# Latent attention: the first half of the next tile's scores ahead of the turning of the current tile's weights

## The reference

```python
C_q  = Q @ Wq_d                                   # 512 -> 64
C_kv = K @ Wkv_d                                  # 512 -> 32
CqWqk = (C_q @ W_qk).reshape(b, n, 16, 32)        # 16 heads
scores = einsum('bnhl,bkl->bhnk', CqWqk, C_kv) / sqrt(32)
attn = softmax(scores)
V_up = (C_kv @ Wv_u).reshape(b, nkv, 16, 32)
out  = einsum('bhnk,bkhd->bnhd', attn, V_up)      # then x = x + tanh(g_xattn[2]) * out
```

## Time and profile before

| what | value |
|---|---|
| median of 3 runs | 2076.41 us (2075.19 to 2080.06) |
| profiled execution: time, span | 2071.11 us, 2069.4 us |
| PE, DVE, ACT, POOL busy over the span | 90%, 79%, 28%, 32% |
| PE, DVE busy of the 1047 us of the first three layers | 907.78 us, 791.88 us |
| latent attention of turn 0: its first exponentials to the last tile's weighted values | 252.33 to 280.19 us |
| waits of ACT's L1188 for DVE's L1630 | 70.0 us in 16 |

### The profile page before, as it was taken

One profiled execution on the slowest core, in us unless ns is written; L12 is line 12 of the kernel. 1 busy time (PEld: TensorE's weight loads), 2 busy tenths in 40 slices (PEclk: granted clock), 3 DMA queues, 4 the chain that ended last, 5 costly groups with the idle time before them and its releaser, 6 DMA issues. The chain is left out here.

```text
span 2069.4 us, 37628 instructions
## 1 busy us (share of the span) xinstructions
PE 1862.5 (90%) x15007; PEld 1043.4 (50%) x15007; DVE 1632.1 (79%) x2908; ACT 586.7 (28%) x1347; POOL 656.3 (32%) x786
## 2 busy tenths in 40 slices
PE   8788889989899898998866899999999999999987
PEld 6344556446554466444533455555555555555543
DVE  4689676986679866798744888888888888888895
ACT  3312233222332223222324122222222222222343
POOL 3500233011420104201124443434343434344563
PEclk9899999999999989999967999999999999999998
DMA  8657204461145601454032211111111111111011
GB/s 245 184 174 211 65 1 144 135 193 41 42 124 156 192 1 42 124 173 113 1 138 72 67 52 47 52 42 52 52 52 52 52 52 52 52 27 32 16 42 52
DMA packets 142300, 176.50 MB, mean 85 GB/s; under 512 B 46768, under 2 KB 82768, under 8 KB 142000
## 3 DMA queue, kind: packets, MB, share of 16 engines
q1 hardware_dynamic: 140112, 172.88, 28.5%
q10 hardware_dynamic: 2016, 1.22, 0.3%
HBM read 131.98 MB, written 42.08 MB: 84 GB/s over the span
## 5 line engine op out<-in xcount | busy, mean ns | idle before, releaser
L1311 POOL TENSOR_TENSOR early_vare<-early_mv,w_eps 128x1 f32<-128x1 f32 x96 | 30.2, 315 | 734.2 <-DVE early_mv L1395 724.3
L2452 POOL TENSOR_TENSOR la_q<-la_straight,la_rot 128x512 f32<-128x512 f32 x128 | 163.3, 1276 | 163.9 <-DVE la_rot L2522 163.9
L440 PE MATMUL la_ps<-w_xTh,w_wqh 128*128 128x512 bf16 x512 | 197.3, 385 | 14.3 <-POOLq L116 8.1
L441 PE MATMUL la_ps<-w_xTl,w_wqh 128*128 128x512 bf16 x512 | 195.8, 382 | 0.0
L442 PE MATMUL la_ps<-w_xTh,w_wql 128*128 128x512 bf16 x512 | 195.7, 382 | 0.0
L440 PE MATMUL la_ps<-w_woh,la_oTh 128*128 128x512 bf16 x512 | 194.0, 379 | 0.0
L441 PE MATMUL la_ps<-w_wol,la_oTh 128*128 128x512 bf16 x512 | 194.0, 379 | 0.0
L442 PE MATMUL la_ps<-w_woh,la_oTl 128*128 128x512 bf16 x512 | 194.0, 379 | 0.0
L2465 POOL TENSOR_TENSOR la_p<-la_s,la_rec 128x256 f32<-128x256 f32 x128 | 90.2, 704 | 273.6 <-DVE la_rec L2543 273.6
L2384 ACT ACTIVATE la_oTh<-la_ps 128x256 bf16<-128x256 f32 x256 | 84.1, 380 | 294.4 <-PE la_ps L2267 294.4
L1552 DVE TENSOR_TENSOR early_products<-early_pR,early_vR 128x4096 f32<-128x4096 f32 x32 | 140.0, 4416 | 16.3 <-DMA early_pR<-scr_p 16.3
(11 more groups left out here) (355 smaller groups left out, 4627.2 us busy)
## 6 DMA issues: line engine op xcount, KB each, us to landing
early_vR<-scr_v SPq DMA_DIRECT2D x128, 257.0 KB, 5.3
early_wkv<-wkv SPq DMA_DIRECT2D x32, 512.0 KB, 4.3
la_v<-v SPq DMA_DIRECT2D x64, 256.0 KB, 4.0
k<-early_ctxt SPq DMA_DIRECT2D x32, 256.0 KB, 3.8
v<-early_ctxt SPq DMA_DIRECT2D x64, 128.0 KB, 2.5
scr_p<-early_weights SPq DMA_DIRECT2D x16, 512.0 KB, 5.0
early_pR<-scr_p SPq DMA_DIRECT2D x32, 256.0 KB, 3.8
w_raw_q<-in_Wq SPq DMA_DIRECT2D x8, 1024.0 KB, 7.5
```

Of the source, the lines that this page charges most:

```text
L440: pe.matmul(out, lh[c], rh[c], start=(first and c == 0), stop=False)
L441: pe.matmul(out, lh[c], rl[c], start=False, stop=False)
L2452: rope_sum.send(pool.tensor_tensor(dst, straight[:, slot, :], rot[:, slot, :], ALU.add))
```

## The change

In each of the three passes j = 0, 1, 2 in each of the four turns, PE issues `scores(j + 1, 0)` ahead of `turn_weights(j)` and no longer behind it. `turn_weights(j)` is now followed directly by `attend(j)`. Nothing else is added or taken away, and every wait stands with its block.

```diff
@@ -1022,9 +1022,9 @@
                         low(j + 2)
                     else:
                         idle_products(6, turn, "prob2", j, 0)
-                    turn_weights(j)
                     if j + 1 < QUAD:
                         scores(j + 1, 0)
+                    turn_weights(j)
                     attend(j)
                     if j + 1 < QUAD:
                         scores(j + 1, 1)
```

## The result

The changed kernel takes 2080.75 us (median of 20 runs, 2074.66 to 2087.59), the one before 2076.49 us beside it (20 runs, 2068.94 to 2080.36 but for one of 9434.22, whose cause is not on record; without it the median is 2076.41). The ratio is 1.0027, with a 95% interval of 1.0017 to 1.0037: slower by 5.6 us, with 3.5 to 7.7 in the interval. Forecast were 2085.8 us and slower by 9.4. The direction is right and the stall is where it was said to be; the amount is smaller than the sum.

What follows compares the result with a forecast made beforehand. DVE and PE were taken as nearly level, PE becoming the bound in tile 2. The tiles' delays reach +2.35 us a turn, 9.4 us over four turns, on the median 2076.41: 2085.8 us, range 2078.5 to 2091.

Steps and rivals of the forecast that it cites:

- Nothing to gain on DVE: In the loop's passes: the first half of the scores already stands before DVE wants it, so bringing it earlier wins nothing.
- The stall of a neighbouring pair: Transposes directly followed by `attend` take 1.98 us start to start against PE's own 0.97: a 1.01 us stall, 12 times.
- Tile 0, +0.44: In tile 0, DVE's second reduction waits for the later second half of the scores: 259.11 instead of 258.67, +0.44 us.
- Tile 1, +0.78 in all: In tile 1, the stall hides from DVE's division, but late scores add 0.10 us to the 0.68 carried in, +0.78.
- Tile 2, +2.35: In tile 2, PE becomes the bound and its 0.41 us slack goes: DVE reduces at 276.25 against 273.90, +2.35 us.
- A sign of the profile that did not come: DVE's reduction waiting for the scores (L977) in tiles 0 to 2, least in tile 1, over 1 us in tile 2.
- Four alike turns: The four turns are alike, so each loses the same 2.35 us, 9.4 us in all.
- I see no transfer that would hide it: Behind `attend(3)`, from layer norm to next turn, engines wait in a chain, so each turn's 2.35 us passes on whole.
- the clock as 3 us either way around nothing: Which block meets a fall of PE's clock from 2.4 to 1.2 GHz shifts, moving the total by 3 us either way.
- Rival A: In the loop, new 1 us gaps drop PE to 1.2 GHz: some 12 us on top, 2098 us; chance 0.05.
- Rival B: In the loop, DVE's own work hides the stall, leaving only 1.8 us in total: 2078.2 us; chance 0.12.
- Rival C: In tile 2, earlier scores fill PE's 0.41 us wait, gaining 1.6 us over four turns: 2072 to 2075; chance 0.05.

## Why the prediction was right, and where its size was off

- **Nothing to gain on DVE.** Right: the first scores half was never waited for before, and is not now.
- **The stall of a neighbouring pair.** Right: 1.98 forecast from tile 3's rows, 1.99 to 2.00 measured, 12 new waits of 0.90.
- **Tile 0, +0.44.** The reduction moved from 258.67 - 252.33 = 6.34 behind the first exponentials to 6.80: +0.46. **Tile 1, +0.78 in all:** 14.65 to 15.55, +0.90. The pair took 2.00 and not 1.98, and `low(3)` held PE for 1.56 (261.16 to 262.72) where I took 1.47. **Tile 2, +2.35:** 21.57 to 24.13, +2.56; the unused products took PE some 1.39 where I took 1.31 (from 268.89 + 1.02 = 269.91, the end of `up`, to 271.30). The loops' 10.3 us lie just above the 8.6 to 10.0 that I gave as bounds: those let only the unused products vary.
- **A sign of the profile that did not come.** DVE's reduction in tile 2 was to wait over 1 us for the scores; it waited 0.28. By my own times the division ends at 275.25 + 0.75 = 276.00, and the scores were to be read from 276.25. The long wait is the division's (1.23, forecast 1.3).
- **Four alike turns.** Right, 2.56 or 2.57 each.
- **"I see no transfer that would hide it", and the clock as 3 us either way around nothing.** This step failed in size. The sum took everything outside the loops as unchanged on the mean, 9.4 us, and measured were 5.6. At an equal mean clock the loss is 8 to 10 us, so the loops' term stands, and a term of about -4 us is missing: PE's mean clock is higher in the changed kernel. The sign of this term could not be had from the rows I used, which showed the clock at one place of one turn. `attend(3)` at 1.69 was in them, and I read it as a risk to the change instead of a cost that the kernel before already bore. That 2080.75 lies inside the range is owed to the 3 us of clock and the room towards B, not to the sum; and that it meets the 2080.5 I had from the profiled execution is luck.
- **Rival A** (the clock falls in the loop) is refuted: the granted clock is 1.00 in all four loops of both profiles of the changed kernel, and filling the stall changed nothing. The rule of the Trainium skill that I named for it ("TensorE: Matmul & The Clock Gate", "A second HAM failure mode: psum-queue depth-cycling") does not bite here, on gaps of 0.90 that stand 8.6 to 8.7 us apart. **Rival B** is refuted by the loops' 2.57. That its 2078.2 lies nearer to 2080.75 than my 2085.8 does is luck; its slack does exist (tile 1's division was not late), but only once a turn. **Rival C** is refuted by the 0.90.

Why the changed kernel meets a higher clock is not settled. The time that PE stood at 1.2 GHz, added up from the granted clock of stretches of 2 us, is 196 and 188 us in the two profiles of before and 183 and 176 us in those of the changed kernel. Only part of this lies right behind the loops, where the clock fell in 4 of 8 turns and in 2 of 8. From the last loop to the end it is 77 and 72 us against 70 and 63. Ahead of the first loop, where the two programs are the same, it is 38 and 48 us against 34 and 41, so single profiles of one kernel differ there by as much as the two kernels do. And the kernel with the move in tiles 0 and 1 has no fall right behind its loops and yet 215 us at 1.2 GHz. Whether it is the way PE is occupied in the last tiles or where the later stages come to lie in time was not told apart.

## What to carry to other kernels

When a block between a producer and its consumer is moved, ask first what its place was hiding: here 1 us of another engine's copying, which the one tile without the block had shown all along. Work the lag through from pass to pass, since two engines that are nearly level hand a stall on to each other. A time that hangs on TensorE's clock should be compared at equal mean clock too before a difference of a few tenths of a per cent is explained, and the clock looked up in every turn and not in one. Here waiting for the halves apart, one wait moved into the middle of `attend`, took 6.7 us off the four changed loops and helped the order of before as well.

## What was not expected of the hardware

The same loss of 2.3 to 2.7 us a turn cost 5.6 us in all (moved scores, clock 0.9534), 7.1 us (TensorE kept busy with unread products, 0.9523) or 15.4 us (an idle TensorE, 0.9443). After an idle TensorE of 2.62 or 4.00 us the clock fell in all eight turns (`attend(3)` 1.93 for 1.14); after 1.27 us, some work and 0.90 us it fell in some turns and not in others of the same kernel; the 0.90 us pieces inside the loops were followed by no fall. Over 95 executions of one and the same kernel the time went down by 12 us for each 0.01 of mean granted clock.
